# Weight and key stages of a graph-attention kernel: matrices turned on TensorE, contiguous stationaries, half-blocks of 16 batches

## The reference, cut to what matters

```
q_exp     = where(row_zero, 0, q[:, None, :])        # q is cond, row_zero: the node's row sums to 0
self_feat = concat([v, q_exp], -1) @ W_self.T + b_self
for d in range(2):
    A = adj or its transpose, first 20 keys
    kv  = self_feat[:, :20]
    qh, kh = self_feat @ Wq[d].T + bq[d],  kv @ Wk[d].T + bk[d]
    aff = einsum('bnhd,bmhd->bnhm', qh, kh) / sqrt(32), masked where A.sum(-1) <= 0, + A @ w_bias + b_bias
    w   = softmax(aff)
    out = einsum('bnhm,bmf,hgf->bnhg', w, kv, Wout[d]) + bout[d]
    output += out
return v + relu(output)
```

## Time and profile before

| what | us |
|---|---|
| median of 3 runs (lowest, highest) | 1953.5 (1951.45, 1953.76) |
| the profiled execution | 1954.26 |
| its span, first to last instruction | 1952.5 |
| first instruction of the keys stage on PE | 79.1 |
| first instruction of the main loop on PE | 408.7 |
| mean granted clock of PE | 0.993 of full |

### The profile page before, as it was taken

How to read it: one execution, slowest core, us unless ns; L and a number is a source line. 1 busy time by engine, 2 the same in 40 slices (tenths; PEclk the granted TensorE clock), 3 DMA queues, 4 the chain that set the end, 5 groups by cost and what they waited for, 6 DMA issues and landing times.

```text
span 1952.5 us, 34072 instructions
## 1 busy us (share of the span) xinstructions
PE 1914.4 (98%) x10888; PEld 1669.7 (86%) x10888; DVE 1332.9 (68%) x1898; ACT 571.3 (29%) x1150; POOL 842.4 (43%) x723
## 2 busy tenths in 40 slices
PE   5899999999999999999999999999999999999999
PEld 3799999988888888888888888888888888888887
DVE  6624223267777777777777777777777777777776
ACT  1231322313232333333333332333223332332231
POOL 1422131134444444444444444444444444544443
PEclk9899999999999999999999999999999999999999
DMA  8423333273444444444444444444444444444421
GB/s 169 90 71 69 93 81 88 72 164 86 118 119 119 118 119 121 125 123 124 126 123 120 120 119 118 118 118 119 122 121 123 121 122 121 121 123 120 124 97 61
DMA packets 240765, 220.89 MB, mean 113 GB/s; under 512 B 57808, under 2 KB 195536, under 8 KB 236624
## 3 DMA queue, kind: packets, MB, share of 16 engines
q1 hardware_dynamic: 236256, 220.28, 42.7%
q10 hardware_dynamic: 4464, 0.02, 0.1%
HBM read 165.44 MB, written 54.79 MB: 113 GB/s over the span
## 4 chain that ended last, share of the span: by engine, by line
PE 77%; DVE 1%; DMA 1%; issue 0%; POOL 0%; ACT 0%; ACTq 0%; SPq 0%; DVEq 0%
PE bank L1306 35%; PE bank L1254 18%; PE bank L1242 12%; PE bank L1278 7%; PE bank L1267 4%; DMA adj<-in_mask_BxSxSx_ik 1%; PE bank L1227 0%; DVE nodes_t L83 0%; DVE qt_main L1065 0%; PE bank L1315 0%; DVE res L1052 0%; DVE sc L1029 0%; DVE res L1050 0%; DVE nodes_t L1001 0%; POOL rc L940 0%
## 5 line engine op out<-in xcount | busy, mean ns | idle before, releaser
L940 POOL TENSOR_TENSOR rc<-nzb,cqg 128x512 f32<-128x512 bf16 x256 | 265.1, 1041 | 412.1 <-DVE qt_main L1065 411.9
L1242 PEld LDWEIGHTS bank<-kbd,qt_main 128*128 128x128 f32 x2048 | 243.5, 192 | 19.5 <-DVE sc L1029 13.6
L1065 DVE SCALAR_TENSOR_TENSOR qt_main<-bank,bq_all,rc 128x512 f32<-128x512 f32 x256 | 189.4, 740 | 90.9 <-PE bank L1306 86.2
L918 POOL TENSOR_TENSOR sc<-sc,mx 128x640 f32<-128x640 f32 x128 | 163.4, 1277 | 199.0 <-DVE mx L1034 199.0
L1242 PE MATMUL bank<-kbd,qt_main 128*128 128x80 f32 x2048 | 247.4, 274 | 0.4 <-DVE sc L1029 0.2
L1152 ACT ACTIVATE wtt<-bank 128x384 f32<-128x384 f32 (+1 forms) x256 | 111.3, 436 | 381.0 <-PE bank L1267 380.9
L1040 DVE TENSOR_REDUCE sm<-sc 128x32 f32<-128x640 f32 x128 | 104.6, 818 | 162.8 <-ACT sc L1144 162.8
L1306 PE MATMUL bank<-nodes_h,wq_h 128*128 128x512 f32 x512 | 210.4, 411 | 0.0
L1306 PE MATMUL bank<-xh_odd,wq_h 128*128 128x512 f32 x512 | 210.4, 411 | 0.0
L1306 PE MATMUL bank<-xh_odd,wq_l 128*128 128x512 f32 x512 | 202.3, 395 | 0.0
L1306 PE MATMUL bank<-nodes_h,wq_l 128*128 128x512 f32 x512 | 202.2, 395 | 0.0
(11 more groups left out here) (120 smaller groups left out, 3915.2 us busy)
## 6 DMA issues: line engine op xcount, KB each, us to landing
rows<-in_x SPq DMA_DIRECT2D x128, 256.0 KB, 4.9
xk<-in_x SPq DMA_DIRECT2D x32, 1024.0 KB, 6.2
res<-c_dram SPq DMA_DIRECT2D x32, 1024.0 KB, 4.6
out<-res SPq DMA_DIRECT2D x128, 256.0 KB, 2.1
adj<-in_mask_BxSxSx_ik SPq DMA_DIRECT2D x32, 440.0 KB, 5.6
adj<-in_mask_BxSxSx_ik SPq DMA_DIRECT2D x128, 110.0 KB
k_dram<-kv_kst SPq DMA_DIRECT2D x64, 160.0 KB, 1.8
v_dram<-kv_vt SPq DMA_DIRECT2D x256, 40.0 KB
```

What stands on the lines that cost most here:

```text
L918: pool.tensor_tensor(s, s, mx[:, b % 2, :].unsqueeze(2).to_broadcast([P, DIRS * H, NG]), ALU.subtract).then_inc(s_shifted, 1)
L940: pool.tensor_tensor(rc[:, c % 2, :].rearrange("p (b n) -> p b n", b=G), nzb[:, par, :].rearrange("p (b n) -> p b n", b=G), cqg[:, par, c, ...
L1065: nc.vector.scalar_tensor_tensor(out=qt[:, c, :], in0=bank[c % 2][:], scalar=bq_all[:, c:c + 1], in1=rc[:, c % 2, :], op0=ALU.add, op1=ALU ...
L1242: mm = nc.tensor.matmul(dst, qt[:, c, b * N:b * N + N], kbd[:, c, :, b * NG:b * NG + NG], start=True, stop=True)
```

## The change

- Weights come in natural rows (2 KB each), one DMA a matrix (four for W_self's x half). PE turns them with 128x128 transposes against the identity into a ring of six banks; ACT and DVE drain each bank: for Wq and W_self's q half one copies, for the matrices that are split ACT casts the high part and DVE subtracts the low part, both from PSUM. POOL makes no low parts of weights any more. The stage has three buffers.
- W_self's x half is turned in the spread order of before (as x still is), its output features and all other matrices in natural order, so the feature stationaries are 128 neighbouring columns.
- The order of the weight stage is rewritten on every engine. ACT issues its bias DMAs first.
- The keys stage goes in eight halves of 16 batches x 20 keys. A half's x is loaded as eight DMAs of 16 partitions (every second one). The next half's sums and features stand between the first six projections of a half on PE; x of the half after that is loaded, turned and split in the same half. `fh` and `fl` have two buffers, by the half's parity. The first half's sums and features stand ahead of the loop.

Weight stage, the new order:

```diff
+def load_half_rows(eng, v, n, par, sem):
+    HB, MH = v["HB"], v["MH"]
+    dst = v["rows"][:, par * MH:par * MH + MH, :]
+    for i in range(NQ):
+        for mh in range(2):
+            src = v["x"][bass.ds(n * HB, HB), mh * MH:mh * MH + MH, i * P:i * P + P]
+            eng.dma_start(dst[Q * i + mh:Q * i + Q:2], src).then_inc(sem, 16)
...
 # SP
+            for r in range(R):
+                sp.dma_start(w1[:, r, :], v["Wself_x"][r * P:r * P + P, :]).then_inc(w1_loaded[r], 16)
+            load_natural(0, v["Wq"][0], wq_loaded[0])
+            load_natural(1, v["Wq"][1], wq_loaded[1])
+            sp.dma_start(cond_rows[0:B], v["cond"]).then_inc(cond_loaded, 16)
+            load_natural(2, v["Wself_q"], w2_loaded)
+            sp.wait_ge(pe_wq, C)
+            load_natural(0, wkv[0], wkv_loaded[0])
...
             sp.wait_ge(pe_fold, DIRS * C)
-            load_block_rows(sp, v, 0, kv_loaded)
+            load_half_rows(sp, v, 0, 0, kv_loaded[0])
+            sp.wait_ge(pe_wkv, C)
+            load_natural(0, wkv[3], wkv_loaded[3])
+            load_half_rows(sp, v, 1, 1, kv_loaded[1])
 # DVE (ws lows and the odd query copies stand ahead of this)
+            for m in range(C, DIRS * C):
+                fold_low(m)
+            matrix_low(0)
+            matrix_low(1)
+            dve.wait_ge(pe_ct, 1)
+            turn_x(0)
+            condition_queries(range(0, C))
+            matrix_low(2)
+            condition_queries(range(C, DIRS * C))
+            matrix_low(3)
+            turn_x(1)
 # PE
+            def turn_rows(t, slot, j):
+                turn_free(t)
+                for r in range(R):
+                    mm = nc.tensor.transpose(turn_bank(t)[:, r * P:r * P + P], stage[:, slot, r, j * P:j * P + P],
+                                             identity[:])
+                return mm
...
+            turn_query(0)
+            fold(0)
+            fold(1)
+            turn_query(1)
+            fold(2)
+            fold(3)
+            (W_self's q half, then cond, turned)
+            fold(4)
+            fold(5)
+            (c: 4 x 4 matmuls, stationary w2t[:, j, jo * P:jo * P + P])
+            fold(6)
+            fold(7)
+            turn_matrix(0)
+            turn_matrix(1)
+            condition_query(0)
+            condition_query(1)
+            turn_matrix(2)
+            condition_query(2)
+            condition_query(3)
+            turn_matrix(3)
+            (rows of c)
```

Keys stage, one half n of each engine (`last`: half 7, `tail`: halves 6 and 7):

```diff
 # SP
+                if not tail:
+                    sp.wait_ge(x_turned, C * (n + 1))
+                    load_half_rows(sp, v, n + 2, par, loaded[par])
+                (8 key stores, then 8 x 4 value stores)
 # DVE
+                if not last:
+                    pick_condition(n + 1)
+                if not tail:
+                    turn_x(blk + 1, n + 2, par)
+                if not last:
+                    nonzero(n + 1, 1 - par)
+                    for j in range(C):
+                        features_out(n + 1, 1 - par, j)
+                (8 value transposes)
 # POOL
+                if not last:
+                    conditions(n + 1)
+                if not tail:
+                    x_lows(n + 2, par)
+                if not last:
+                    features_low(n + 1, 1 - par)
 # ACT
+                for j in range(C):
+                    key_out(n, par, j)
+                    if not tail:
+                        x_cast(n + 2, par, j)
+                for j in range(C):
+                    key_out(n, par, C + j)
+                    if not last:
+                        feature_high(n + 1, 1 - par, j)
+                (8 value_out)
 # PE
+            def features(n, par, jo):
+                three(slot_bank(1 - par, FEAT_SLOT[jo]),
-                          lambda j: chunk_columns(ws_h[:, j, :], jo), lambda j: chunk_columns(ws_l[:, j, :], jo),
+                      lambda j: ws_h[:, j, jo * P:jo * P + P], lambda j: ws_l[:, j, jo * P:jo * P + P],
+                      lambda j: x_cols(xh, j, par), lambda j: x_cols(xl, j, par)).then_inc(pe_feat, 1)
...
+                pe.wait_ge(f_low, C * (n + 1))
+                project(0)
+                project(1)
+                next_sums()
+                project(2)
+                next_features(0)
+                project(3)
+                next_features(1)
+                project(4)
+                next_features(2)
+                project(5)
+                next_features(3)
+                for p in range(6, 2 * NK):
+                    project(p)
```

## The result

| kernel | median us (lowest, highest) |
|---|---|
| before, 4 runs | 1953.4 (1951.5, 1953.8) |
| changed, 4 runs | 1937.7 (1936.5, 1938.0) |

The ratio is 0.9921, 95% interval 0.9906 to 0.9937. The change gains 15.6 us where 30.4 were forecast; 1937.7 lies 0.7 us above the range. The profiled execution has a span of 1936.1 us.

What follows compares the result with a forecast made beforehand. PE was taken as the bound, busy 98% of the span and never idle in the keys stage. Stages 76.0 + 298.0 + 3.3 + 1543.8 gave a 1921.1 us span, forecast as 1923 us, range 1915 to 1937.

Steps and rivals of the forecast that it cites:

- Features, -33.1 us: Keys stage: contiguous stationaries take all 384 feature matmuls from 0.2327 to 0.1466 us each, -33.1 us.
- The column rule: Rival for feature loads: a load is priced by its number of columns alone, so no gain, 1956; 2%.
- Ramp, 2.6 us: Keys stage, first half-block: projection 0 waits for all four low parts, 2.6 us of PE idle, once.
- Weight stage, start at 76.0: Rewritten weight stage ends earlier: keys stage starts at 76.0 instead of 79.1, -3.1 us; bounds -8 and +6.
- The waypoints: Predicted times along the weight stage, from fold 0 at 14.0 to the last fold pair ending at 52.9.
- The clock behind transposes, taken at nothing: Weight stage: low clock behind stretches of transposes priced at nothing; bounds nothing or +6 net on the stage's end.
- The pinch: Keys stage, projection 4 waits for key 1 behind cast 0: 0.5 us in each of halves 1 to 5, 2.5 us.
- SP's start, +3.24 taken: Within the pinch: SP starts the x loads, behind value stores, 3.24 us after the half's start.
- A load's issue, 0.57 taken: Within the pinch: each of eight x loads takes SP 0.57 us, the eighth issued at 7.2.
- Landing 2.0 taken: Within the pinch: x loads land 2.0 us after issue, as 64 KB loads of the same 512 B rows.
- a rival's place in the weight stage: Rival: transposes leave PE at the low clock, weight stage +6 instead of -3.1, +9, 1932; 13%.
- late loads: Rival in the keys stage: the pinch costs 3.1 us instead of 0.5, five times, +13, 1936; 16%.

Runs made afterwards that it cites:

- e5: Kernel before with one edit: feature stationaries are 128 neighbouring columns instead of every fourth; 1920.5 us, ratio 0.9834.
- e1: Changed kernel with x of half n+2 turned, cast and split behind the features of half n+1 on DVE, ACT and POOL; 1923.8 us, ratio 0.9851.
- e3: Changed kernel with SP's half-blocks written out eight times with constant addresses instead of a loop; 1924.4 us, ratio 0.9851.
- e6: Changed kernel with the feature stationaries back to every fourth column; one run, 1959.1 us.
- e7: Changed kernel with x turned, cast and split behind the next half's features and SP's half-blocks written out; 1921.1 us, ratio 0.9835.
- e4: Changed kernel with each x load written to 16 neighbouring partitions instead of every second one; one run, 1929.6 us.
- e2: Changed kernel with each cast of x put one key evacuation later on ACT; one run, 1933.8 us.
- e8: Changed kernel's weight stage with the keys stage of before in whole blocks, contiguous feature stationaries, first block's x turned whole; 1920.3 us, ratio 0.9834.
- e9: e8 with the first block's x turned on DVE behind the first condition queries and third matrix's lows; 1916.9 us, ratio 0.9818.

## Why the prediction was wrong

- **Features, -33.1 us: right.** e5 measures it alone, -32.9. The column rule that was weighed against it (the Trainium skill, "TensorE: Matmul & The Clock Gate", "LDWEIGHTS (loading the stationary operand)") does not hold for this stride: 329 ns against 187 for one shape and one number of columns.
- **Ramp, 2.6 us: 2.33.** Right, for the idle. The clock behind it was not priced: it stayed at full here, but fell in e1, e3, e6 and e7, 1.5 to 1.6 us each.
- **Weight stage, start at 76.0: 76.23.** Close, but partly by luck. The waypoints held within a microsecond or two: fold 0 at 15.2 (14.0), the last pair ending at 52.4 (52.9). A transpose takes 0.12 at full clock and 0.23 at the low one, not 0.14, and a wait of 2.25 us ahead of the second condition queries was missed. Seven profiled executions share this order of the stage (this one, e1 to e4, e6, e7), and their keys stages start at 74.14 to 79.06. The clock moves them: the first fold pair takes 7.23 us (e1, e4, e6) or 8.96 to 9.53 (here, e2, e3, e7), the second condition queries 3.84 (here, e2, e4) or 5.4 to 5.5 (e1, e3, e6, e7). Behind the old weight stage it started at 79.10 in one execution and at 76.91 in the other (e5). So a gain of 3.1 us in this stage is not shown.
- **The clock behind transposes, taken at nothing: right as far as these stretches go.** The pair at 25.73 stands behind 16 transposes and takes 7.15; the queries at 55.94 stand behind 32 and take 3.78, at full pace. In e1 the clock even comes back to full at 14.0 us, when PE had run nothing but transposes. The rule of the Trainium skill, "TensorE: Matmul & The Clock Gate", "Part 4: PE-mode transpose", would have put what follows transposes at the low clock; these traces don't show that.
- **The pinch, "I take 0.5 each, 2.5 us": this step failed.** The place was right (projection 4, key 1 behind cast 0), and in e1, which undoes it, and e6, which gives it 2.1 us more room, it behaves as worked out. The size was 10.5 us of idle, and 6.7 on top (5.9 at the low clock, the rest at the stalls' edges), 17.2 for 2.5. It came in four halves, not five: half 1, whose loads stand behind stores outside the loop, had no stall. Four parts of it, for half 3:
  - SP's start, +3.24 taken, +5.80 found. I read the boundary at 162.15, behind block 0, which stands outside the loop. In the loop a value store took SP 0.50 us instead of 0.43, four a projection, 2.0 us against PE's 1.76: SP falls behind by 0.24 us a projection, 1.9 us over eight. The trace before had it: 64 stores in 27.7 us in block 0 and in 31.5 in block 1. It was free there, since nobody waited for the loads behind it. e3 takes it away (+3.1).
  - A load's issue, 0.57 taken, 0.75 found in the loop. I took the pitch of four loads into 32 neighbouring partitions; the step of two adds 0.26 to an issue (e4).
  - Landing 2.0 taken, 2.4 found. Small.
  - The clock. I gave it a rival's place in the weight stage and none behind the stalls, though the earlier trace rows show the low clock behind idle. The rival "late loads" had the longest stalls nearly right (3.1 each) and lies at 1936, nearest of all, but by luck: it priced landing instead of SP's lateness, five stalls instead of four, and no clock.

  With these numbers key 1 is free at 15.35 instead of 11.0, while PE could have gone on at 11.73: the stall is 3.5 us of idle.
- This closes the gap. By spans, with the 1921.1 of the forecast's sum: 1921.1 - 2.5 + 17.2 = 1935.8, against 1936.1. That 1923 - 2.5 + 17.2 gives 1937.7 to the tenth is rounding that came out well.

What stays open: why the clock falls behind some stalls and not behind others. It fell behind idle of 3.52, 3.16 and 2.78 here, of 2.67 and 2.42 in e2 and of 2.36 and 1.83 in e4, and not behind 2.84 in e2, 2.33 here and 2.18 in e4. The wait ahead of projection 0 is the plainest case: 2.31 to 2.33 us in seven executions, with a fall in e1, e3, e6 and e7 and none here, in e2 and in e4. The length of the idle alone does not order them.

No pair of kernels differs in the half-block order alone, but the traces price the keys stage by itself, from its first matmul to that of the main loop. Without stalls in halves 2 to 5 it takes 299.8 to 300.1 us in half-blocks (e1, e3, e7) and 296.4 to 297.7 in blocks (e5, e8, e9). The half-blocks cost 2 to 4 us: they have the wait ahead of projection 0 and the low clock behind it, and the blocks had no idle that they could take away.

## What to carry to other kernels

A queue that nobody waits for can be late at no cost; before something is hung behind it, read how late it runs in the stretch that repeats, not at a boundary outside the loop. A stall on PE is to be priced with the low clock that may follow it: here 1.5 to 2.6 us or nothing, for stalls of 1.8 to 3.5. And of a change in many parts, the one with the largest term is worth trying alone: one line (e5) gave 32.9 us, the whole change 15.6. That line leaves out the matching order of the key and value matrices; with it, in e8, the time is the same, 1920.3.

## What was not expected of the hardware

- In a loop, with addresses from registers, a small DMA costs its queue more: a value store 0.48 to 0.50 us instead of 0.43, an x load 0.75 instead of 0.64. e3 takes away loop and registers at once; which of them costs is not shown.
- A load into every second partition costs 581 ns to issue, into 16 neighbouring ones 317 (e4).
- A weight load of 128x128 with a stride of four elements takes 325 to 330 ns, without it 187 to 190.
- The clock comes back to full in a stretch of transposes alone (e1), and behind one and the same wait of 2.3 us it falls in four executions and stays in three.
